# A four-stage transformer kernel on one core: a depth-routed layer written with overlapping batches, and the products of two rotary attention steps issued together

## The chip, the core and the metric

The kernel runs on one core of a Trainium2 chip. The metric is the device time of one execution in microseconds (us), lower is better. Six kinds of work appear in the profile: PE (TensorE's matmuls), PEld (TensorE's weight loads), DVE (VectorE), ACT (ScalarE), POOL (GpSimd) and SP, which issues the DMAs.

## What is computed

The input x is 4 sequences (B) of 1024 tokens (T) with 128 channels (D), float32. Four stages follow each other, each with a residual and a layer norm:

```python
x = layernorm(x + linear_attention(x))        # 16 heads
x = layernorm(x + switch_attention(x))        # 8 heads, 5 experts, top 3
x = layernorm(x + rotary_attention(x))        # 16 heads of 8 channels, full softmax
x = layernorm(x + depth_routed_ffn(x))

def depth_routed_ffn(x, w_r, b_r, W1, b1, W2, b2):
    weights = x @ w_r + b_r                    # one number a token
    threshold = top_k(weights, 512)[-1]        # per sequence
    selected = weights > threshold
    hidden = gelu(x @ W1 + b1)                 # 128 -> 512
    blk = hidden @ W2 + b2                     # 512 -> 128
    return where(selected, blk, x)
```

The change touches the third and the fourth stage only.

## The kernel before

Each stage is a function with its own block: all five engines run their own list of instructions, meet at its end, and POOL clears the stage's semaphores. The order on each engine is written out by hand; waits are semaphores.

**Rotary attention (`rotary_lead`).** A batch has 16 heads in groups of 4; a group has 2 pairs of heads and 8 key tiles, so a batch has 64 steps (pair and key tile `kt`) and the stage 256. A step has two score units (c = 0 and 1, one for each half of the queries). A score unit (L2072) is two matmuls for the two heads of the pair, each on 32 rows of the array, into one of three buffers `unit_b` of two PSUM banks each; score unit u goes where unit u-3 was, so it waits until ACT's exponential of unit u-3 is done. ACT's exponential (L2020) reads 128x1024 scores and writes `probs`, two buffers by step. The products of a step (L2087) are four matmuls on four column groups of the array (each recorded as two, so eight records), which read `probs` and add into the one bank `acc_b`. After 8 steps DVE copies `acc_b` (L2182), PE turns the copy (`turn`, L2099) and DVE divides. Between the steps lie "pieces" of the neighbouring batches: the projections q, k (with their swapped forms) and v of the next batch, each half a batch, and the transposition and output projection of the batch before. All of them use one bank, `piece_b`, which DVE must have read before the next piece is made. DVE normalizes the batch before (`norm`) right behind the last output projection. PE's order in a step is: score unit c=1 of this step, c=0 of the next, the products of the step before, then a turn or a piece, if one is due. The positions come from `PIECE_STEPS`, `TURN` and `NORM_AT`.

**Depth-routed layer (`depth_ffn`).** A loop over the 4 batches. SP loads the batch from the SBUF tensor `r1` into `xs` once more. PE transposes it (L2320), ACT copies it (`xT`, L2296), PE makes the router's row with the router vector repeated over 128 columns (L2326), ACT adds the bias (`w_row`, L2300), PE turns it into a column (L2339), and makes the hidden layer in four blocks (L2333), of which ACT takes the gelu (L2305). DVE counts, for each of 8 token tiles, how many weights are as large (L2366). PE makes the output channels by tokens (L2344), ACT adds the bias (L2307), PE transposes back (L2350), and DVE selects (L2382), normalizes (L66 to L85) and SP stores. The transposition of the next batch waits for ACT's L2307, and the counting of the next batch stands behind the norm of this one on DVE.

## Time and profile before

| | us |
|---|---|
| median of 3 runs (2033.87 to 2038.4) | 2034.81 |
| the profiled execution, its own time | 2035.62 |
| its span, first to last instruction | 2033.8 |
| rotary stage's exponentials, first start to last end | 514.8 |
| depth-routed layer, first load to the last store's issue | 112.3 |

The span is that of the profiled execution; 1.8 us lie around it. A time in a row counts from the span's start. In a timeline the first number is the start and the second the length of a merged stretch; what stands in brackets is how long the engine had been idle before it and what ended that.

### The profile page before, as it was taken

How to read it: one execution, taken by the hardware profiler on the slowest of the kernel's cores; microseconds unless marked ns; L12 is line 12 of the kernel's file. 1: busy time of each engine (PE TensorE's matmuls, PEld its weight loads, DVE VectorE, ACT ScalarE, POOL GpSimd, SP SyncE). 2: the span in 40 equal slices, each digit the busy share in tenths (PEclk: the TensorE clock that was granted, in tenths of full speed). 3: DMA queues.
4: the chain of work that ended last, by engine and by line, in shares of the span. 5: the costliest groups of instructions: out<-in, count | busy, mean ns of one | idle time of the engine just before them, and what ended most of it. 6: DMA issues, size and time to landing. Idle time of an engine off the chain costs nothing. (4 is left out here: it accounts for less than half of the span.)

```text
span 2033.8 us, 25515 instructions
## 1 busy us (share of the span) xinstructions
PE 1784.7 (88%) x8756; PEld 815.7 (40%) x8756; DVE 1163.4 (57%) x1924; ACT 1273.6 (63%) x2424; POOL 920.5 (45%) x512
## 2 busy tenths in 40 slices
PE   7888469999999999999999998529999999999386
PEld 3433245444545445554555552212333332333142
DVE  6998597986668776687765662331313223120287
ACT  1121215677676767767677677409999999999132
POOL 4566306788866788667887688400000000000000
PEclk8998689999999999999999999769999999999698
DMA  2000000000000000000000000022311212210011
GB/s 69 1 1 0 24 20 15 16 20 20 11 20 11 20 14 17 20 10 20 11 20 20 11 10 1 0 97 81 104 42 60 86 43 65 81 43 1 23 36 36
DMA packets 28808, 61.01 MB, mean 30 GB/s; under 512 B 4528, under 2 KB 15232, under 8 KB 28672
## 3 DMA queue, kind: packets, MB, share of 16 engines
q1 hardware_dynamic: 28672, 59.29, 9.0%
q8 instruction: 74, 1.21, 0.2%
q14 instruction: 62, 0.51, 0.1%
HBM read 38.31 MB, written 18.87 MB: 28 GB/s over the span
## 5 line engine op out<-in xcount | busy, mean ns | idle before, releaser
L707 POOL TENSOR_TENSOR b_psum<-b_psum,b_probs 128x1024 f32<-128x1024 f32 x192 | 460.7, 2400 | 172.4 <-ACT b_probs L847 165.8
L2020 ACT ACTIVATE c_probs<-banks 128x1024 f32<-128x1024 f32 x512 | 484.0, 1040 | 67.2 <-PE banks L2072 48.6
L1225 DVE TENSOR_TENSOR b_gated<-banks,b_g 128x480 f32<-128x480 f32 x512 | 314.2, 656 | 226.2 <-PE banks L949 221.3
L847 ACT ACTIVATE b_probs<-banks 128x1024 f32<-128x1024 f32 x256 | 254.2, 1019 | 216.1 <-PE banks L982 215.3
L949 PE MATMUL banks<-b_w,b_xh 128*128 128x480 f32 x1024 | 351.9, 398 | 33.4 <-DVE b_gated L1225 19.3
L1233 DVE TENSOR_REDUCE b_tok<-b_gated 128x192 f32<-128x960 f32 x256 | 281.5, 1139 | 0.5
L2087 PE MATMUL banks<-c_probs,c_vg 128*32 128x512 f32 x2048 | 273.9, 607 | 5.3 <-DVE c_acc L2182 3.5
L982 PE MATMUL banks<-b_qq,b_kk 64*128 64x512 f32 x1024 | 262.6, 622 | 14.2 <-DVE b_gated L1225 10.1
L818 ACT ACTIVATE b_share<-b_o,b_picked 128x64 f32<-128x64 f32 x1080 | 268.8, 339 | 0.0
L1014 PE MATMUL banks<-b_probs,b_tok 128*64 128x512 f32 x1024 | 252.4, 614 | 2.4 <-ACT b_probs L847 2.4
L949 PEld LDWEIGHTS banks<-b_w,b_xh 128*128 128x128 f32 x1024 | 194.3, 190 | 115.7 <-issue 39.6
L2004 POOL COPY c_vg<-c_v 128x64 f32<-128x64 f32 x64 | 12.3, 238 | 471.3 <-PE banks L2087 342.7
L2072 PE MATMUL banks<-c_queries,c_keys 32*128 32x512 f32 x1024 | 206.0, 468 | 18.9 <-DMA c_queries<-c_heads 17.2
L949 PE MATMUL banks<-b_w,b_xl 128*128 128x480 f32 x512 | 195.6, 382 | 0.0
L2072 PEld LDWEIGHTS banks<-c_queries,c_keys 32*128 32x128 f32 x1024 | 84.0, 184 | 219.0 <-ACT c_probs L2020 183.0
L718 POOL TENSOR_TENSOR b_z<-b_z,b_share 128x1280 f32<-128x1280 f32 x54 | 157.5, 2917 | 0.0
L1014 PEld LDWEIGHTS banks<-b_probs,b_tok 128*64 128x64 f32 x1024 | 62.8, 138 | 175.9 <-issue 143.6
L982 PEld LDWEIGHTS banks<-b_qq,b_kk 64*128 64x128 f32 x1024 | 87.2, 186 | 111.9 <-issue 59.4
L2182 DVE COPY c_acc<-banks 128x512 f32<-128x512 f32 x32 | 22.1, 691 | 191.1 <-PE banks L2087 190.9
L281 POOL TENSOR_TENSOR a_qscan<-a_scan,a_q 128x1024 f32<-128x1024 f32 x36 | 89.0, 2478 | 89.6 <-DVE a_scan L440 89.6
L707 POOL TENSOR_TENSOR b_psum<-b_probs 128x1024 f32<-128x1024 f32 x32 | 76.4, 2388 | 74.9 <-ACT b_probs L847 74.9
L399 PE MATMUL banks<-a_qscan,a_sel 128*128 128x512 f32 x128 | 73.3, 702 | 32.2 <-POOL a_qscan L281 32.1
(226 smaller groups left out, 1863.0 us busy)
## 6 DMA issues: line engine op xcount, KB each, us to landing
b_raw_w<-in_L_ffn_W SPq DMA_DIRECT2D x32, 480.0 KB, 3.2
c_heads<-c_split SPq DMA_DIRECT2D x24, 512.0 KB
c_keys<-c_heads SPq DMA_DIRECT2D x16, 512.0 KB, 3.8
c_queries<-c_heads SPq DMA_DIRECT2D x16, 512.0 KB, 5.1
c_heads<-c_split SPq DMA_DIRECT2D x8, 384.0 KB
a_xs<-in_L_attn_x SPq DMA_DIRECT2D x4, 512.0 KB, 8.3
d_xs<-r SPq DMA_DIRECT2D x4, 512.0 KB, 2.9
out<-d_yo SPq DMA_DIRECT2D x4, 512.0 KB, 3.2
```

The lines of the kernel that those rows point to most:

```text
L707: nc.gpsimd.tensor_tensor(psum[:, par, :], prev, probs[:, i % 4, :], ALU.add).then_inc(psum_rdy, 1)
L718: nc.gpsimd.tensor_tensor(zf, zf, sf, ALU.add).then_inc(z_rdy[half], 1)
L818: nc.scalar.activation(dst[:, e, :], o[:, t, :], ACT.Copy, scale=picked[:, b % 2, t, h * E + e:h * E + e + 1]).then_inc(share_rdy, 1)
L847: nc.scalar.activation(probs[:, i % 4, :], score_b[i % 2], ACT.Exp).then_inc(exp_rdy, 1)
L949: last = nc.tensor.matmul(proj_b[u % WAYS][:, 0:HALF_W], a[:, x_of % 2, t * P:(t + 1) * P], w[:, par, part, j, :], start=(i == 0), stop=(i ...
L982: last = nc.tensor.matmul(score_b[i % 2][:, lo:hi], kk[rows, par, (side + i) % 2, i // 2 * P:(i // 2 + 1) * P], qq[rows, par, :], start=Tr ...
L1014: last = nc.tensor.matmul(acc_b[DH * half:DH * half + DH, :], tok[:, n % 4, 2, i, :], probs[:, i % 4, lo:hi], start=(i == 0), stop=(i == N ...
L1225: nc.vector.tensor_tensor(shape(gated[:, t % 2, j, :]), shape(proj_b[u % WAYS][:, 0:HALF_W]), g.unsqueeze(2).broadcast_to([P, 3, HD2, E]), ...
L1233: nc.vector.tensor_reduce(tok[:, n % 4, :, t, :].rearrange("p j (f d) -> p f j d", f=2), gated[:, t % 2, :, :].rearrange("p f (j d e) -> p ...
L2020: nc.scalar.activation(probs[:, step % 2, c, :, :], unit_b[u % NU], ACT.Exp, scale=float(HD) ** -0.5).then_inc(exp_rdy, 1)
L2072: last = nc.tensor.matmul(unit_b[u % NU][:, s, :], keys[at:at + 32, par, kt * P:(kt + 1) * P], queries[at:at + 32, par, c * HALF:(c + 1) * ...
L2087: last = nc.tensor.matmul(acc_b[at:at + 32, :], vg[:, par, kt, 2 * pp + s, :], probs[:, kt % 2, half, s, :], start=(kt == 0), stop=(kt == ...
```

## The change

Rotary attention becomes `rotary_twos`: the products of two steps stand next to each other in PE's list, behind the score units of every even step; `probs` has four buffers where it had two; turns and pieces stand at odd steps; the norm of the batch before stands behind step 14.

```diff
@@ -1822,7 +1822,7 @@
-def rotary_lead(nc, x, out, ps, ident, I, flag, tag):
+def rotary_twos(nc, x, out, ps, ident, I, flag, tag):
@@ -1841,10 +1841,10 @@
-    TURN = 2
-    NORM_AT = 13
+    TURN = 3
+    NORM_AT = 14
-    PIECE_STEPS = [i + 1 if i % NT == TURN else i for i in range(3, 3 * (NZ + NX) + 3, 3)]
+    PIECE_STEPS = [i for i in range(5, STEPS * NG, 2) if i % NT != TURN][:NZ + NX]
@@ -1860,7 +1860,7 @@
-        probs = sb("probs", [P, 2, 2, 2, HALF])
+        probs = sb("probs", [P, 4, 2, 2, HALF])
@@ -2013,11 +2013,11 @@
-                act.wait_ge(pv_done, ONE + STEPS - 1 + step)
+                act.wait_ge(pv_done, ONE + STEPS - 3 + step)
-                    nc.scalar.activation(probs[:, step % 2, c, :, :], unit_b[u % NU], ACT.Exp, scale=float(HD) ** -0.5).then_inc(exp_rdy, 1)
+                    nc.scalar.activation(probs[:, step % 4, c, :, :], unit_b[u % NU], ACT.Exp, scale=float(HD) ** -0.5).then_inc(exp_rdy, 1)
@@ -2084,7 +2084,7 @@
-                        last = nc.tensor.matmul(acc_b[at:at + 32, :], vg[:, par, kt, 2 * pp + s, :], probs[:, kt % 2, half, s, :],
+                        last = nc.tensor.matmul(acc_b[at:at + 32, :], vg[:, par, kt, 2 * pp + s, :], probs[:, kt % 4, half, s, :],
@@ -2112,10 +2112,9 @@
-                    if i:
-                        products(b, i - 1)
-                    elif not first:
-                        products(b - 1, BS - 1)
+                    if i % 2 == 0 and step:
+                        for back in (2, 1):
+                            products(*((b, i - back) if i else (b - 1, BS - back)))
@@ -2123,7 +2122,8 @@
-            products(B - 1, BS - 1)
+            for back in (2, 1):
+                products(B - 1, BS - back)
```

The depth-routed layer becomes `depth_lead`, written out for the four batches. PE transposes straight from `r1`, without the load into `xs`. The transposition, the router's row and its column for batch b+1 stand between the hidden blocks of batch b; the router's column is eight transpositions of one row each. The output comes out as tokens by channels: the hidden layer is the stationary operand and W2 the moving one (32 matmuls of 128 columns where there were 8 of 512), so that the transposition back and ACT's bias pass are gone. POOL makes x times its weight plus b2 for the selected tokens (three passes over 128x1024, `keep`) and iterates the inverse roots for batches 0 to 2; ACT writes their normalized output. DVE counts for batch b+1 (`choose`) before it gathers batch b. Many buffers are doubled.

```diff
-def depth_ffn(nc, x, out_dram, ps, ident, I):
+def depth_lead(nc, x, out_dram, ps, ident, I):
...
+        piece_b = [ps[:, 0, :], ps[:, 1, :]]
+        hid_b = [ps[:, i:i + 2, :].rearrange("p a n -> p (a n)") for i in (2, 4)]
+        blk_b = [ps[:, 6, :], ps[:, 7, :]]
...
+            sp.dma_start(wr[:, :], I["L1_ffn_w_r"]).then_inc(r_in, 16)
+            sp.dma_start(br[:, :], I["L1_ffn_b_r"].rearrange("(o n) -> o n", o=1).broadcast_to([P, 1])).then_inc(r_in, 16)
+            sp.dma_start(w1[:, :], I["L1_ffn_W1"]).then_inc(w1_in, 16)
+            sp.dma_start(b1[:, :], I["L1_ffn_b1"]).then_inc(w1_in, 16)
+            sp.dma_start(b2[:, :], I["L1_ffn_b2"].rearrange("(o n) -> o n", o=1).broadcast_to([P, D])).then_inc(b2_in, 16)
+            sp.dma_start(w2[:, :, :], I["L1_ffn_W2"].rearrange("(n p) c -> p n c", p=P)).then_inc(w2_in, 16)
...
+            def keep(b):
+                if b == 0:
+                    pool.wait_ge(b2_in, 16)
+                pool.wait_ge(chosen, 2 * b + 2)
+                if b >= 2:
+                    pool.wait_ge(y_rdy, NT * (b - 1))
+                nc.gpsimd.tensor_tensor(kept[:, b % 2, :, :], x[:, b * NT:(b + 1) * NT, :], weight[:, b % 2, :].unsqueeze(2).broadcast_to([P, NT, D]), ALU.mult).then_inc(scaled, 1)
+                nc.gpsimd.tensor_tensor(shifts[:, :, :], b2[:, :].unsqueeze(1).broadcast_to([P, NT, D]), sel[:, b % 2, :].unsqueeze(2).broadcast_to([P, NT, D]), ALU.mult).then_inc(scaled, 1)
+                pool.wait_ge(scaled, 2 * b + 2)
+                nc.gpsimd.tensor_tensor(kept[:, b % 2, :, :], kept[:, b % 2, :, :], shifts[:, :, :], ALU.add).then_inc(kept_rdy, 1)
...
+            def inverse_roots(b):
+                pool.wait_ge(moments, MOMENT_STEPS * (b + 1))
+                st = Steps(pool, newton, NEWTON_STEPS * b)
+                var, half_step = tmp[:, 0, :], tmp[:, 1, :]
+                for _ in range(3):
...
+            keep(0)
+            for b in range(B):
+                if b + 1 < B:
+                    keep(b + 1)
+                    inverse_roots(b)
...
+            def hidden(b, n):
+                act.wait_ge(hid_ps, NB * b + n + 1)
+                if b and n == 0:
+                    act.wait_ge(blk_ps, 2 * b)
+                nc.scalar.activation(hid[:, n, :], hid_b[n % 2], ACT.Gelu, bias=b1[:, n:n + 1]).then_inc(hid_sb, 1)
...
+            def finish_norm(b):
+                act.wait_ge(newton, NEWTON_STEPS * (b + 1))
+                if b >= 2:
+                    act.wait_ge(out_done[b - 2], 16)
+                for t in range(NT):
+                    nc.scalar.activation(yo[:, b % 2, t, :], y[:, b % 2, t, :], ACT.Identity, bias=shift[:, t:t + 1], scale=rs[:, t:t + 1]).then_inc(normed, 1)
...
+            copy_x(0)
+            copy_rows(0)
+            act.wait_ge(w1_in, 16 * 2)
+            for b in range(B):
+                hidden(b, 0)
+                if b + 1 < B:
+                    copy_x(b + 1)
+                hidden(b, 1)
+                if b + 1 < B:
+                    copy_rows(b + 1)
+                hidden(b, 2)
+                hidden(b, 3)
+                if b:
+                    finish_norm(b - 1)
...
+            def turn_x(b):
+                for half in range(2):
+                    if b and half == 0:
+                        pe.wait_ge(col_sb, b)
+                    if b and half == 1:
+                        pe.wait_ge(row_sb, 2 * b)
+                    for j in range(4):
+                        last = nc.tensor.transpose(piece_b[half][:, j * P:(j + 1) * P], x[:, b * NT + 4 * half + j, :], ident[:, :])
+                    last.then_inc(turned, 1)
...
+            def router_column(b):
+                pe.wait_ge(row_sb, 2 * b + 2)
                 for t in range(NT):
-                    last = nc.tensor.transpose(tr_ps[:, t * P:(t + 1) * P], xs[:, t, :], ident[:, :])
-                last.then_inc(xT_ps, 1)
-                pe.wait_ge(xT_sb, b + 1)
-                pe.wait_ge(y_rdy, ONE + b)
+                    last = nc.tensor.transpose(piece_b[0][:, t:t + 1], w_row[0:1, b % 2, t * P:(t + 1) * P], ident[0:1, 0:1])
+                last.then_inc(col_ps, 1)
...
+            def contract(b):
+                if b == 0:
+                    pe.wait_ge(w2_in, 16)
+                pe.wait_ge(hid_sb, NB * b + NB)
+                for half in range(2):
+                    if b:
+                        pe.wait_ge(y_rdy, NT * (b - 1) + NT // 2 * (half + 1))
+                    for j in range(4):
+                        t = 4 * half + j
+                        for n in range(NB):
+                            last = nc.tensor.matmul(blk_b[half][:, j * P:(j + 1) * P], hid[:, n, t * P:(t + 1) * P], w2[:, n, :], start=(n == 0), stop=(n == NB - 1))
+                    last.then_inc(blk_ps, 1)
...
+            turn_x(0)
+            router_row(0)
+            router_column(0)
+            for b in range(B):
+                expand(b, 0)
+                if b + 1 < B:
+                    turn_x(b + 1)
+                expand(b, 1)
+                if b + 1 < B:
+                    router_row(b + 1)
+                expand(b, 2)
+                expand(b, 3)
+                if b + 1 < B:
+                    router_column(b + 1)
+                contract(b)
...
+            def choose(b):
                 dve.wait_ge(col_ps, b + 1)
-                nc.vector.tensor_copy(w_col[:, :], row_b.rearrange("p (t r) -> p t r", r=P)[:, :, 0]).then_inc(col_sb, 1)
+                nc.vector.tensor_copy(w_col[:, b % 2, :], piece_b[0][:, 0:NT]).then_inc(col_sb, 1)
                 dve.wait_ge(col_sb, b + 1)
+                dve.wait_ge(row_sb, 2 * b + 2)
+                if b:
+                    dve.wait_ge(chosen, 2 * b)
                 for t in range(NT):
-                    if t >= 2:
-                        dve.wait_ge(steps, b * V_STEPS + t - 1)
-                    st.done(nc.vector.tensor_scalar(ge[:, t % 2, :], w_row[:, :], w_col[:, t:t + 1], None, ALU.is_ge, ALU.add,
-                                                    accum_out=count[:, t:t + 1]))
+                    if NT * b + t >= 2:
+                        dve.wait_ge(counts, NT * b + t - 1)
+                    nc.vector.tensor_scalar(ge[:, t % 2, :], w_row[:, b % 2, :], w_col[:, b % 2, t:t + 1], None, ALU.is_ge, ALU.add,
+                                            accum_out=count[:, t:t + 1]).then_inc(counts, 1)
+                dve.wait_ge(counts, NT * (b + 1))
+                if b >= 2:
+                    dve.wait_ge(y_rdy, NT * (b - 1))
+                    dve.wait_ge(scaled, 2 * (b - 1))
+                nc.vector.tensor_scalar(sel[:, b % 2, :], count[:, :], float(K), None, ALU.is_lt).then_inc(chosen, 1)
+                dve.wait_ge(chosen, 2 * b + 1)
+                nc.vector.tensor_scalar(weight[:, b % 2, :], sel[:, b % 2, :], -1.0, 2.0, ALU.mult, ALU.add).then_inc(chosen, 1)
...
+            def gather(b, half):
+                dve.wait_ge(blk_ps, 2 * b + half + 1)
+                if half == 0:
+                    dve.wait_ge(kept_rdy, b + 1)
+                    dve.wait_ge(chosen, 2 * b + 1)
+                    if b >= 2:
+                        dve.wait_ge(normed, NT * (b - 1))
+                for j in range(4):
+                    t = 4 * half + j
+                    nc.vector.scalar_tensor_tensor(y[:, b % 2, t, :], blk_b[half][:, j * P:(j + 1) * P], sel[:, b % 2, t:t + 1], kept[:, b % 2, t, :], ALU.mult, ALU.add).then_inc(y_rdy, 1)
...
+            def moment_guess(b, st):
                 st.settle()
-                st.link(nc.vector.tensor_scalar(sel[:, :], count[:, :], float(K), None, ALU.is_lt))
-                st.link(nc.vector.tensor_scalar(keep[:, :], sel[:, :], -1.0, 2.0, ALU.mult, ALU.add))
-                dve.wait_ge(x_in, 16 * b + 16)
+                if b:
+                    dve.wait_ge(newton, NEWTON_STEPS * b)
+                    dve.wait_ge(normed, NT * b)
...
+            choose(0)
+            for b in range(B):
+                if b + 1 < B:
+                    choose(b + 1)
+                st = Steps(dve, moments, MOMENT_STEPS * b)
+                for half in range(2):
+                    gather(b, half)
+                    moment_stats(b, st, half)
+                moment_guess(b, st)
+            last_norm(B - 1)
...
-        depth_ffn(nc, r1, out_dram, ps, ident, I)
+        depth_lead(nc, r1, out_dram, ps, ident, I)
```

The places on which the prediction rests are all in PE's and DVE's lists. PE in the rotary stage, around a turn (c_queries and c_keys are the score units' operands, c_probs the products'), before:

```order
L2072 MATMUL banks<-c_queries,c_keys 128x512 x4
L2087 MATMUL banks<-c_probs,c_vg 32x512 x4
L2099 MATMUL banks<-ident,c_acc 128x128 x4
L2072 MATMUL banks<-c_queries,c_keys 128x512 x4
L2087 MATMUL banks<-c_probs,c_vg 32x512 x4
```

The same place in the changed kernel:

```order
L2087 MATMUL banks<-c_probs,c_vg 32x512 x8
L2072 MATMUL banks<-c_queries,c_keys 128x512 x4
L2099 MATMUL banks<-ident,c_acc 128x128 x4
L2072 MATMUL banks<-c_queries,c_keys 128x512 x4
L2087 MATMUL banks<-c_probs,c_vg 32x512 x8
L2072 MATMUL banks<-c_queries,c_keys 128x512 x8
```

A step's two score units and its products alternated; now eight product matmuls stand together, and between two such groups eight score matmuls, with a turn (or a piece) in their middle where one is due.

PE in the depth-routed layer, before, the loop's body from the last hidden block (d_xT, d_w) to the transposition back (REGISTER_ALU rows belong to waits against a counter):

```order
L2333 MATMUL banks<-d_xT,d_w 128x512 x2
L2344 MATMUL banks<-d_hid,d_w 128x512 x4
L2342 REGISTER_ALU
L2344 MATMUL banks<-d_hid,d_w 128x512 x2
L2342 REGISTER_ALU
L2344 MATMUL banks<-d_hid,d_w 128x512 x2
L2347 REGISTER_ALU
L2350 MATMUL banks<-ident,d_blk 128x128 x8
```

The changed kernel, batch 0 from its first hidden block to its output:

```order
L2412 MATMUL banks<-d_xT,d_w 128x512 x2
L2387 MATMUL banks<-ident,r 128x128 x8
L2412 MATMUL banks<-d_xT,d_w 128x512 x2
L2396 MATMUL banks<-d_xT,d_wr 128x512 x2
L2412 MATMUL banks<-d_xT,d_w 128x512 x4
L2402 MATMUL banks<-ident,d_w_row 128x1 x8
L2426 MATMUL banks<-d_w,d_hid 128x128 x32
```

L2387, L2396 and L2402 belong to the next batch; the output's matmuls (L2426) went from 8 to 32, and no transposition follows them.

DVE in the changed layer, its first rows:

```order
L2451 COPY d_w_col<-banks 128x8
L2459 TENSOR_SCALAR d_ge,d_count<-d_w_row,d_w_col 128x1024 x8
L2465 TENSOR_SCALAR d_sel<-d_count 128x8
L2467 TENSOR_SCALAR d_weight<-d_sel 128x8
L2479 SCALAR_TENSOR_TENSOR d_y<-banks,d_sel,d_kept 128x128 x4
L2487 BN_STATS d_stats<-d_y 128x6 x4
```

The first four rows come twice (batches 0 and 1) before the gathering of batch 0, which is cut here to its first half.

## Rows read from the trace of the kernel before

**Rows 1.** Busy times by engine in a stretch, then clock, DMA share, GB/s.

```profile
1924.00:2033.80 109.80, 82.17 (x240) 40.43 (x240) 81.84 (x284) 30.80 (x28) 0.00 (x0) 0.87 0.10 34
```

**Rows 2.** Timeline of ACT, rotary stage: start, length, exponentials in it.

```profile
1370.88 3.77 ACT L2020 ACTIVATE c_probs<-banks 128x1024 f32<-128x1024 f32 x4 [36.42 <-PE banks L2072]
...
1378.05 16.62 ACT L2020 ACTIVATE c_probs<-banks 128x1024 f32<-128x1024 f32 x18 [0.51 <-PE banks L2087]
...
1493.19 14.79 ACT L2020 ACTIVATE c_probs<-banks 128x1024 f32<-128x1024 f32 x16 [0.18 <-PE banks L2087]
...
1624.40 14.79 ACT L2020 ACTIVATE c_probs<-banks 128x1024 f32<-128x1024 f32 x16 [0.17 <-PE banks L2087]
```

**Rows 3.** Timeline of the last rotary batch, which holds no projections.

```profile
1863.25 14.79 ACT L2020 ACTIVATE c_probs<-banks 128x1024 f32<-128x1024 f32 x16 [0.18 <-PE banks L2087]
...
1865.24 0.18 PEld L2072 LDWEIGHTS banks<-c_queries,c_keys 32*128 32x128 f32 x2 [0.29 <-ACT c_probs L2020]
...
1865.67 1.07 PE L2087 MATMUL banks<-c_probs,c_vg 128*32 128x512 f32 x8
...
1878.21 7.44 ACT L2020 ACTIVATE c_probs<-banks 128x1024 f32<-128x1024 f32 x8 [0.16 <-PE banks L2087]
```

**Rows 4.** Timeline of batch 1, a turn and an output projection.

```profile
1522.22 0.66 PE L2099 MATMUL banks<-ident,c_acc 128*128 128x128 f32 x4
...
1522.80 0.73 PE L2072 MATMUL banks<-c_queries,c_keys 32*128 32x512 f32 x4
...
1524.46 0.73 PE L2072 MATMUL banks<-c_queries,c_keys 32*128 32x512 f32 x4
...
1525.12 1.06 PE L2087 MATMUL banks<-c_probs,c_vg 128*32 128x512 f32 x8
...
1526.12 1.16 PE L2057 MATMUL banks<-c_wo,c_aoT 128*128 128x128 f32 x8
1527.21 0.73 PE L2072 MATMUL banks<-c_queries,c_keys 32*128 32x512 f32 x4
...
1527.75 1.03 ACT L2020 ACTIVATE c_probs<-banks 128x1024 f32<-128x1024 f32 x1 [0.29 <-PE banks L2072]
```

**Rows 5.** Timeline of the switch stage, products on two column groups.

```profile
1104.78 1.94 PE L1014 MATMUL banks<-b_probs,b_tok 128*64 128x512 f32 x8
...
1106.64 3.04 PE L1053 MATMUL banks<-b_zT,b_wo 128*128 128x512 f32 x6
```

**Rows 6.** Timeline of DVE, the norm in batch 1: first and last part.

```profile
1528.04 1.65 DVE L66 BATCH_NORM_STATS2 c_stats<-c_y 128x6 f32<-128x128 f32 x8
...
1532.73 2.14 DVE L85 TENSOR_SCALAR r<-c_y,c_mv,c_rs 128x128 f32<-128x128 f32 x8
```

**Rows 7.** Groups of the depth-routed layer: busy, mean ns, idle before and releasers.

```profile
L2366 DVE TENSOR_SCALAR_CACHE_REDUCE d_ge<-d_w_row,d_w_col 128x1024 f32<-128x1024 f32 x32 | 38.7, 1275 | 0.1
L2333 PE MATMUL banks<-d_xT,d_w 128*128 128x512 f32 x64 | 28.8, 592 | 0.0
...
L2307 ACT ACTIVATE d_blk<-banks,d_b 128x1024 f32<-128x1024 f32 x4 | 4.5, 1114 | 23.0 <-PE banks L2344 23.0
```

**Rows 8.** Timeline of the depth-routed layer: its start, its end.

```profile
1916.47 0.57 SPq L2262 DMA_DIRECT2D d_xs<-r  x1
...
1924.19 1.96 PE L2320 MATMUL banks<-ident,d_xs 128*128 128x128 f32 x8 [17.43 <-POOL d_wr_rep L2287]
...
1927.25 3.44 PE L2326 MATMUL banks<-d_xT,d_wr_rep 128*128 128x512 f32 x4 [1.10 <-ACT d_xT L2296]
...
2028.73 0.39 SPq L2273 DMA_DIRECT2D out<-d_yo  x1
```

**Rows 9.** Timeline of the linear stage: POOL's inverse roots, ACT's normalized output.

```profile
149.43 0.20 POOL L267 TENSOR_TENSOR a_rs<-a_tmp,a_rs 128x8 f32<-128x8 f32 x1
149.72 2.16 POOL L264 TENSOR_TENSOR a_tmp<-a_rs 128x8 f32<-128x8 f32 x1
...
171.27 3.19 ACT L323 ACTIVATE r<-a_y,a_shift,a_rs 128x128 f32<-128x128 f32 x8
```

**Rows 10.** Group of POOL, rotary stage: one pass over 128x1024.

```profile
L1994 POOL TENSOR_TENSOR c_xb<-r,c_b_all 128x1024 f32<-128x1024 f32 x4 | 9.5, 2369 | 0.0
```

200 lines of the change are left out of this document (95 added, 105 removed).

## The prediction

> **What bounds the kernel now.** I read the page's slices first (which stages keep PE full), then the timelines of ACT and of PE in the two changed stages. The other two stages keep their instructions and get no term.
>
> In the rotary stage ACT is the slower engine as long as PE has only its steps: 16 exponentials stand back to back in 14.79 us [rows 3], and with the last one's 1.03 [rows 4] that is (14.79 - 1.03)/15 = 0.918 us each, 1.84 a step. PE needs less: two score units 0.66 (1524.46 to 1525.12), the products 1.00 (1525.12 to 1526.12), so 1.66 [rows 4]. The reader should see in [rows 3] that the second score unit of a step (1865.24) starts 0.05 after the second exponential ends (1863.25 + 0.918 + 1.03 = 1865.20): PE waits there for ACT. Where a projection stands between (1.09, from 1526.12 to 1527.21 [rows 4]) PE needs 2.75 and ACT waits. That is why 128 exponentials with projections take 131.2 us (1493.19 to 1624.40) [rows 2], and without them 16 take 14.96.
>
> The depth-routed layer is bound by no engine: PE is busy 82.2 of 109.8 us, DVE 81.8 [rows 1]. It is a chain, (2028.73 - 1924.19)/4 = 26 us a batch [rows 8]; ACT's bias pass alone waits 23.0 us in four rounds for PE's output [rows 7], and the count of the next batch (8 x 1.275, [rows 7]) stands behind the norm.
>
> **Rotary stage, the change.** Nothing is added but order and buffers. Two things follow.
>
> First, what PE saves. The products of one step are two passes over four column groups, 1.00. The nearest row for two steps together is a run of four passes over two column groups, 1104.78 to 1106.64 = 1.86 [rows 5], against 2 x 1.00. So a pass is (1.86 - 1.00)/2 = 0.43 and the change of array shape 0.14. The score side loses one change as well: four units in a row would take less than 2 x 0.66. I take 1.86 for the pair of products; bounds 1.72 (nothing but the streaming, 4 x 0.43) and 2.00 (two of today's).
>
> Second, what PE's list now makes ACT wait for. Follow the ring of three score buffers. Score unit u=2i+2 waits for exponential 2i-1. Behind it stand the products of two steps, and only then unit 2i+3. So from the start of exponential 2i-1 to the start of exponential 2i+3: 1.03 + 0.05 (end to score unit, above) + 0.43 (score unit to products, 1865.24 to 1865.67 [rows 3]) + 1.86 (products) + 0.54 (score unit to exponential, 1527.21 to 1527.75 [rows 4]) = 3.91 us for four exponentials, where ACT needs 4 x 0.918 = 3.67. Before, the same ring was 1.03 + 0.05 + 0.43 + 1.00 + 0.54 = 3.05 and hidden. The ring becomes the bound: I use 3.90, with bounds 3.76 and 4.04.
>
> A turn or a transposition (0.58, 1522.22 to 1522.80 [rows 4]) is hidden in it: 1.86 + 0.66 + 0.58 + 0.66 = 3.76 of PE. A projection (1.09) is not: 1.86 + 0.66 + 1.09 + 0.66 = 4.27, or about 4.24 for a q or k piece; 0.34 over the ring. There are 10 + 12 + 12 + 2 = 36 of these in the four batches: 12.2 us. The norm takes DVE 6.83 us (1528.04 to 1532.73 + 2.14) [rows 6], now behind the piece of step 13: the first transposition's copy then ends some 8.4 us after that piece, and PE comes to the second one (step 17), which needs the same bank, after about 7.1. That is 1.3 in each of three batches, 3.9. The slow start stays (six exponentials from 1370.88 to 1378.05 are 7.2 where 5.5 would do, 1.7 [rows 2]).
>
> Sum: 511 gaps = 127.75 x 3.90 = 498.2, + 1.0 (the last one) + 12.2 + 3.9 + 1.7 = 517.0 us, against 514.8 now (1370.88 [rows 2] to 1878.21 + 7.44 [rows 3]). The stage loses 2.2 us: what the projections cost less (131.2 a batch becomes about 130) is given back in the steps without them (119.7 a batch becomes 124.8). Bounds from the ring alone: -16 and +20.
>
> **Depth-routed layer, the change.** The new path, in the trace's time, if the block starts where it does (1916.47 [rows 8]):
> - The router's row needs the first two loads, not all seven. PE starts at 1924.19 today, when all have landed [rows 8]; the second load is issued about 1 us in. I take 1920.7 (between 1918 and 1924); the transposition (1.96 [rows 8]) lies ahead of it. Row 3.44 at the clock of [rows 8], ACT's half 0.6 (half of a 1.1 pass [rows 7]), column about 0.9 (an estimate, eight small transpositions): 1925.7.
> - To the first output: four hidden blocks at 1.73 (four passes of 0.43), transposition 1.09, row 1.73, then the last gelu 1.2 (a pass of that shape is 1.114 [rows 7]): 10.9. Contraction of batch 0 starts at 1936.6.
> - The contraction is 32 matmuls of 128 columns; the nearest row has four in 1.09 with a change of array shape in it [rows 4], so 8 x 0.9 = 7.3, at most 8 x 1.09 = 8.7 (now 6.9). A round of PE is 7.3 + 10.9 = 18.2. DVE needs 8 x 1.275 = 10.2 for a count [rows 7] and about 6 for the rest (the norm's 6.83 without its last 2.14 and the small steps, and 8 selections), POOL 3 x 2.37 [rows 10] + 14 x 0.29 [rows 9] = 11.2, ACT 4 x 1.1 + 4 x 0.6 + 3.2 = 10: PE bounds the round. Contraction of batch 2 starts at 1973.0, of batch 3 at 1988.4 (no next batch in it: 15.4).
> - The end hangs on the other engines. The count of batch 3 starts just before the contraction of batch 2 and ends at 1982.9; POOL's three passes to 1990.0, inverse roots of batch 2 to 1994 (I take 1996), ACT's eight writes 3.2 [rows 9]: 1999.2. Only then may DVE aggregate batch 3 (it gathered by 1998): aggregation and twelve small steps 3.1 (now 1528.04 + 1.65 to 1532.73 = 3.04 for nearly the same [rows 6]), ACT's four writes 1.7: 2004.0.
>
> The last store is issued at 2004.1 instead of 2028.73 [rows 8]: -24.6. Bounds: contraction at 8.7 and each POOL pass a third longer give -17, an earlier start -28.
>
> **Sum.** 2035.62 (the profiled execution's own time) - 24.6 + 2.2 = 2013.2. That execution lies 0.8 above the median of the runs, so about 2012.5; I say 2013.
>
> **Rivals.**
> - *The ring does not bind; PE's saving counts.* The stage would run at ACT's pace, and only the pairs with a projection at PE's: 470.1 (511 x 0.918 + 1) + 3.9 + 1.7 + 36 x 0.57 = 496.2, 18.6 less than now; 1992 in all. For it: the products' 1.00 has 0.14 beyond the two passes, and the score units' 0.66 some 0.2, once less in each pair. Against it: the wait at 1865.24 stands just there, and the ring hides only products of 3.67 - 2.05 = 1.62. The Trainium skill (TensorEngine Tiling, Key Properties) says that changing the tiling mode drains the engine; by that alone, fewer changes are a gain, and it says nothing of who waits for the scores in the meantime. 0.12.
> - *The products of two steps take twice what one takes* (2.00). Ring 4.04, + 17.9: 2031. Against it are [rows 5]. 0.10.
> - *Slower than before: POOL's small steps stall.* A 128x8 step takes 0.20 as a rule and once 2.16 [rows 9]. The round leaves POOL 18.2 - 11.2 = 7.0 us, 3.6 such stalls; beyond, each costs 1.96 on the way to ACT's writes and the next aggregation. The gain of 22.4 is spent by 11.4 more over three batches; with all 14 stalled in each of them the time is 2013 + 3 x (27.4 - 7.0) = 2074. Decides: more than some 7 of 14. Against it: DVE was scanning there, and here it compares one tensor with a column. The Trainium skill (SBUF — State Buffer) has the two engines block each other only where DVE reads two SBUF tensors or runs in a two-port mode, which speaks against it too. 0.06.
> - *The forecast*, with its terms within their bounds: 0.72, own range 2003 to 2024.
>
> **How the numbers follow.** About 0.2% (4 us) is what a measurement can tell here. The range 1996 to 2031 leaves out the first rival and the third. Faster holds the forecast, the first rival and nearly all of the second: 0.91; same 0.04 (second with the layer at -17); slower 0.05.
>
> **What would show it.** Right: products of L2087 with 16 records in some 1.9 us; exponentials in groups of four with about 0.2 idle before the fourth's successor, released by PE's scores; 16 of them in 15.6 us in the last batch (now 14.96), but a batch with projections near 130; contractions 18 us apart, last store issued about 88 us after the stage's start. Wrong: ACT back to back in the last batch (first rival); POOL steps of 2 us on the chain (third); an output contraction over 9 us; a lower granted clock in the rotary stage, where PE will pause near 0.9 us in each pair of steps.

## The result, and the profile after

The changed kernel takes 2012.72 us (median of 4 runs, 2010.14 to 2014.0); the kernel before took 2035.43 in runs beside it. The ratio is 0.9885 with a 95% interval from 0.987 to 0.9899: 1.15% faster. The forecast was 2013. The profiled execution took 2014.0 us, with a span of 2012.1, 21.7 less than before.

ACT in the rotary stage, the changed kernel (start, length, exponentials in the stretch, in brackets the idle time ahead of it):

```profile
1372.41 6.52 ACT L2020 ACTIVATE c_probs<-banks 128x1024 f32<-128x1024 f32 x7 [36.80 <-PE banks L2072]
1380.58 19.37 ACT L2020 ACTIVATE c_probs<-banks 128x1024 f32<-128x1024 f32 x20 [1.65 <-PE banks L2072]
...
1519.96 11.57 ACT L2020 ACTIVATE c_probs<-banks 128x1024 f32<-128x1024 f32 x12 [0.28 <-PE banks L2072]
...
1649.47 11.56 ACT L2020 ACTIVATE c_probs<-banks 128x1024 f32<-128x1024 f32 x12 [0.28 <-PE banks L2072]
...
1799.09 86.83 ACT L2020 ACTIVATE c_probs<-banks 128x1024 f32<-128x1024 f32 x89 [0.40 <-PE banks L2072]
```

The stage's 512 exponentials last from 1372.41 to 1885.92 (1799.09 + 86.83), 513.5 us; before they lasted 514.8 ([rows 2, 3]). A batch is 129.5 (1519.96 to 1649.47) where it was 131.2. Executions differ by more than the 1.3 us of the stage: the same rotary stage took 513.5 to 516.2 us in six profiles (here, e1, e8, e9, e10, e12), the old one 514.8 and 515.0 (before, e2). In the part of the last batch that holds no projections, 89 exponentials take 86.83, so 16 take 15.6 where they took 14.96 [rows 3]. PE in that batch, a pair of steps with a turn in it:

```profile
1843.08 0.50 PE L2072 MATMUL banks<-c_queries,c_keys 32*128 32x512 f32 x2 [0.65 <-ACT c_probs L2020]
1843.51 1.92 PE L2087 MATMUL banks<-c_probs,c_vg 128*32 128x512 f32 x16
1845.36 0.73 PE L2072 MATMUL banks<-c_queries,c_keys 32*128 32x512 f32 x4
1846.02 0.66 PE L2099 MATMUL banks<-ident,c_acc 128*128 128x128 f32 x4
```

The reader should see that the score unit at 1843.08 waits for ACT, and that behind it PE gives 1.85 us (1843.51 to 1845.36) to the products before it makes the next one. PE has become the less loaded engine. The two rows give its busy time first, ACT's as the fourth and the granted clock as the sixth number, in the last batch before and after:

```profile
1779.00:1885.00 106.00, 104.72 (x710) 32.30 (x708) 16.93 (x65) 103.35 (x112) 3.94 (x9) 1.00 0.06 21
1779.00:1886.00 107.00, 94.73 (x699) 32.92 (x698) 16.42 (x65) 102.83 (x109) 4.17 (x9) 1.00 0.06 21
```

The clock stayed at 1.00 although PE now pauses in each pair, so that sign of being wrong did not come.

The depth-routed layer, PE and the last of the other engines, from a timeline (the pieces of SP are DMA issues):

```profile
1917.45 0.35 SPq L2264 DMA_DIRECT2D d_wr<-in_L_ffn_w_r  x1
...
1920.73 3.78 PE L2396 MATMUL banks<-d_xT,d_wr 128*128 128x512 f32 x4 [1.16 <-DMA d_br<-in_L_ffn_b_r]
...
1926.23 3.78 PE L2412 MATMUL banks<-d_xT,d_w 128*128 128x512 f32 x4
1929.81 1.91 PE L2387 MATMUL banks<-ident,r 128*128 128x128 f32 x8
1931.51 2.35 PE L2412 MATMUL banks<-d_xT,d_w 128*128 128x512 f32 x4
...
1999.37 1.12 DVE L2479 SCALAR_TENSOR_TENSOR d_y<-banks,d_sel,d_kept 128x128 f32<-128x128 f32 x4 [1.54 <-PE banks L2426]
...
2004.53 1.65 ACT L2374 ACTIVATE d_yo<-d_y,d_shift,d_rs 128x128 f32<-128x128 f32 x4 [4.61 <-DVE d_shift L2511]
...
2006.61 0.51 SPq L2277 DMA_DIRECT2D out<-d_yo  x1
```

From the first load's issue to the last store's it is 89.2 us; it was 112.3 [rows 8]. In the chain that ended last, the four contractions (L2426) stand where PE starts each of them:

```profile
1940.31 7.38 PE banks L2426 x64
...
1957.19 1.12 ACT d_hid L2347
1958.36 7.41 PE banks L2426 x64
...
1976.43 7.41 PE banks L2426 x64
...
1991.92 7.43 PE banks L2426 x64
```

A round is 18.05 us. The chain runs through PE, with one gelu in each round, and not through DVE or POOL until the last gather; but DVE is idle for only some 1.6 us of a round, so DVE's own list is close behind as a limit. The 21.7 us of the span are: 23.1 from the layer, 1.3 from the exponentials, and against them 1.5 ahead of the first exponential (1372.41 for 1370.88), 0.7 between the last one and the layer, and 0.4 behind the last store (the parts are rounded). Some of this belongs to the execution and not to the change: in eight other profiles of the new layer in this order (e2 to e7, e11 and e12) it took 85.6 to 87.7 us where this one shows 89.2.

### The profile page after: what moved, and what is told of

It is laid out like the page before. It is cut to its first block and busy times, and to the rows that moved or that the text cites. A ratio compares the mean times of both kernels' runs of the same rounds, so it can differ in the third digit from the quotient of the medians.

```text
span 2012.1 us, 25633 instructions
## 1 busy us (share of the span) xinstructions
PE 1750.1 (87%) x8916; PEld 836.6 (42%) x8916; DVE 1149.1 (57%) x1834; ACT 1280.4 (64%) x2456; POOL 953.7 (47%) x565
## 5 line engine op out<-in xcount | busy, mean ns | idle before, releaser
L949 PE MATMUL banks<-b_w,b_xh 128*128 128x480 f32 x1024 | 353.3, 399 | 33.5 <-DVE b_gated L1225 19.4
L982 PE MATMUL banks<-b_qq,b_kk 64*128 64x512 f32 x1024 | 263.7, 625 | 14.7 <-DVE b_gated L1225 10.0
L2087 PE MATMUL banks<-c_probs,c_vg 128*32 128x512 f32 x2048 | 247.7, 601 | 0.3 <-DVE c_acc L2182 0.2
L2072 PE MATMUL banks<-c_queries,c_keys 32*128 32x512 f32 x1024 | 191.4, 464 | 49.8 <-ACT c_probs L2020 31.9
L2072 PEld LDWEIGHTS banks<-c_queries,c_keys 32*128 32x128 f32 x1024 | 79.7, 183 | 217.9 <-ACT c_probs L2020 183.7
```

Of the source, the lines that this page charges most:

```text
L949: last = nc.tensor.matmul(proj_b[u % WAYS][:, 0:HALF_W], a[:, x_of % 2, t * P:(t + 1) * P], w[:, par, part, j, :], start=(i == 0), stop=(i ...
L982: last = nc.tensor.matmul(score_b[i % 2][:, lo:hi], kk[rows, par, (side + i) % 2, i // 2 * P:(i // 2 + 1) * P], qq[rows, par, :], start=Tr ...
L2072: last = nc.tensor.matmul(unit_b[u % NU][:, s, :], keys[at:at + 32, par, kt * P:(kt + 1) * P], queries[at:at + 32, par, c * HALF:(c + 1) * ...
L2087: last = nc.tensor.matmul(acc_b[at:at + 32, :], vg[:, par, kt, 2 * pp + s, :], probs[:, kt % 4, half, s, :], start=(kt == 0), stop=(kt == ...
```

## The experiments

All ratios are to the kernel before, run on the same chip in the same job; its medians were 2037.19, 2038.74 and 2037.60 us in the three jobs.

| kernel | us | ratio, 95% interval |
|---|---|---|
| e1_rotary_alone | 2039.98 | 1.0014, 1.0002 to 1.0025 |
| e2_depth_alone | 2012.26 | 0.9883, 0.986 to 0.9906 |
| e3_twice_before | 2046.28 | 1.0031, 1.0011 to 1.005 |
| e4_twice_middle | 2025.49 | 0.9932, 0.991 to 0.9954 |
| e5_single_four | 2006.16 | 0.9838, 0.9815 to 0.9861 |
| e6_norm_late | 2012.0 | 0.9867, 0.9851 to 0.9884 |
| e7_mixed | 2013.67 | 0.9881, 0.9864 to 0.9898 |
| e8_no_lead | 2036.77 | 0.9985, 0.9974 to 0.9996 |
| e9_count_behind | 2025.13 | 0.9939, 0.9924 to 0.9954 |
| e10_router_ahead | 2026.94 | 0.9943, 0.9928 to 0.9959 |
| e11_four_late | 2001.48 | 0.9827, 0.9813 to 0.984 |
| e12_after_again | 2014.2 | 0.9876, 0.986 to 0.9892 |

### Each part alone

The kernel before with the new rotary function:

```diff
-        rotary_lead(nc, r2, r1, ps, ident, I, flag, "c_")
+        rotary_twos(nc, r2, r1, ps, ident, I, flag, "c_")
         depth_ffn(nc, r1, out_dram, ps, ident, I)
```

> The kernel before with the changed rotary stage alone; the depth-routed layer stays as it was. Theory (the ring of three score buffers bounds the stage at 3.90 us a pair of steps, which gives back what the projections cost less): no change that can be measured, 2034 us, the exponentials again over some 513.5 us. Rival (PE's saved changes of array shape are a gain of the whole change): 2016 us.

And with the new depth-routed layer:

```diff
         rotary_lead(nc, r2, r1, ps, ident, I, flag, "c_")
-        depth_ffn(nc, r1, out_dram, ps, ident, I)
+        depth_lead(nc, r1, out_dram, ps, ident, I)
```

> The kernel before with the changed depth-routed layer alone; the rotary stage stays as it was. Theory: all of the gain, 2012.5 us, the last store issued 89 us after the layer's first load. Rival (a part of the gain belongs to the rotary stage): 2018 us or more.

2039.98 and 2012.26 us. By the ratio the rotary part costs 0.14%, 2.8 us beside the kernel before on the same chip, with an interval from 0.4 to 5. In e1's profile the stage itself takes 516.0 us, 1.2 more than before, and 2.9 lie ahead of the stage, in code that the change doesn't touch; so that 2.8 is near the forecast of 2.2 is partly chance. The layer is the whole gain (85.7 us in e2's profile). The rival in which PE's saving counts is gone. e1 came out 6 us above its expectation: 2.5 are its longer slow start (below), and the kernel before was some 2 slower on this chip than in the first runs; the rest is not settled.

### Where the rotary stage's ring runs

A score unit computed a second time right behind itself costs PE some 0.23 us. In e3 it is the one that stands ahead of the products, within the ring of three score buffers that the prediction drew; in e4 the one in the middle, outside of it.

```diff
-                for s in range(2):
+                for s in (0, 1, 0, 1) if c == 0 and step % 2 == 1 else (0, 1):
```

> The changed kernel with one score unit of each pair of steps computed twice into the same banks: the one right ahead of the two products (the same result, 0.22 us more of PE). It lies inside the ring from an exponential's end over the products to the next score unit. Theory (ring): the ring grows from 3.90 to 4.12 in all 128 pairs, + 28 us, 2041 us. Rival (ACT bounds the stage, or PE does with slack): under + 10 us. If PE's total work bounds the stage, this run and the next cost the same.

```diff
-                for s in range(2):
+                for s in (0, 1, 0, 1) if c == 0 and step % 2 == 0 else (0, 1):
```

> The changed kernel with another score unit of each pair computed twice: the second one behind the products, before the turn or piece. The same 0.22 us of PE, outside the ring. Theory (ring): nothing in pairs without a projection, 0.22 in the 36 with one and about 0.08 in those with a turn, + 10 us, 2023 us; the last batch stays at 15.6 us for 16 exponentials. Rival (PE's total work bounds the stage): + 28 us like the run before.

Timelines of ACT in the last batch, first e3, then e4:

```profile
1875.44 3.77 ACT L2020 ACTIVATE c_probs<-banks 128x1024 f32<-128x1024 f32 x4 [0.36 <-PE banks L2072]
1879.58 3.77 ACT L2020 ACTIVATE c_probs<-banks 128x1024 f32<-128x1024 f32 x4 [0.37 <-PE banks L2072]
```

```profile
1865.82 15.47 ACT L2020 ACTIVATE c_probs<-banks 128x1024 f32<-128x1024 f32 x16 [0.22 <-PE banks L2072]
1881.51 15.48 ACT L2020 ACTIVATE c_probs<-banks 128x1024 f32<-128x1024 f32 x16 [0.22 <-PE banks L2072]
```

The same matmuls, inside the ring, make a pair of steps 4.14 us (1875.44 to 1879.58), 0.24 over the 3.90; outside of it 3.92 (1865.82 to 1881.51, a quarter). By the ratios e3 costs some 30 us over the changed kernel (0.0146 x 2037) and e4 some 10, against 28 and 10 expected. What e4 costs it costs where projections stand, since there PE's own work sets the pace. (Each profile also has one wait of 2 to 2.5 us behind the norm, with PE at its lower clock, that the changed kernel's has not.) So away from the projections it is the ring that paces the stage: shown.

### Single products with four buffers, and the norm's place

e5 has the new layer, but issues the products after every step, as before, and has the turns, the pieces and the norm where they were before. Of the rotary change it keeps the four buffers (the edit is shown against the kernel before):

```diff
-        probs = sb("probs", [P, 2, 2, 2, HALF])
+        probs = sb("probs", [P, 4, 2, 2, HALF])
-                act.wait_ge(pv_done, ONE + STEPS - 1 + step)
+                act.wait_ge(pv_done, ONE + STEPS - 3 + step)
```

> The changed kernel's depth-routed layer, but in the rotary stage the products are issued after every step again, as before the change, with four buffers for the exponentials' results in place of two. The theory (the pair's products stand between two score units and so make the ring of three score buffers 3.90 us per two steps; single products leave it at 3.05, hidden by ACT's 3.67, and what is left of a loss before the change is the wait of each turn's exponential for a buffer, 0.28) expects 16 exponentials of the last batch in about 14.7 us (15.6 in the changed kernel, 14.96 before), the batches with projections between 127 and 131 us, and 1997 to 2006 us in all. The rival (the order of the products is not what paces the stage, 0.975 us per exponential is ACT's own pace there or the score units') expects 15.6 and the changed kernel's time, 2012.

It took 2006.16 us. ACT in its last batch:

```profile
1801.78 81.69 ACT L2020 ACTIVATE c_probs<-banks 128x1024 f32<-128x1024 f32 x89 [1.83 <-PE banks L2072]
```

89 exponentials in 81.69 us (86.83 in the changed kernel): 0.918 each, ACT's own pace, with no wait at a turn. Against e2, which differs from it in the two buffers alone, the ratio falls from 0.9883 to 0.9838, some 9 us, though the intervals just touch; in the two profiles the exponentials of the stage take 509.2 instead of 515.0, so 6 us are seen in the stage. The buffers were the useful half of the rotary change, and the order of the products, with the places that it needs, took back what they gave. The time lies just above the range's upper end; the row shows 1.83 us lost behind the norm, for which e6 and e11 were made. PE waits only 1.11 us there, for DVE's copy, and then works at its lower clock (a step's products take 1.94 us for 1.06). e6 is the changed kernel with

```diff
-    NORM_AT = 14
+    NORM_AT = 46
```

> The changed kernel with the norm of the finished batch on DVE at step 46 of a batch in place of step 14, where no turn or transposition waits for DVE's copies any more. The theory (the norm makes a transposition's copy late and PE waits 1.57 us for it in each of three batches) expects the three waits gone and 4 to 5 us less than the changed kernel: 2008. The rival (PE's wait is covered by the ring of score buffers all the same) expects 2012.

2012.0 us, its ratio 0.9867 against 0.9885 and 0.9876 for the changed kernel: no gain that can be told. The wait at the norm (PE's 1.57 us, in two of the three batches and not in all three as I had expected) is gone, and e6's batch shrinks to 128.1 us, but its start was slower by nearly as much. Timeline of ACT in e6, its start and one point of batches 1 and 3:

```profile
1373.22 6.52 ACT L2020 ACTIVATE c_probs<-banks 128x1024 f32<-128x1024 f32 x7 [36.77 <-PE banks L2072]
1382.18 3.77 ACT L2020 ACTIVATE c_probs<-banks 128x1024 f32<-128x1024 f32 x4 [2.44 <-PE banks L2072]
1387.81 12.74 ACT L2020 ACTIVATE c_probs<-banks 128x1024 f32<-128x1024 f32 x13 [1.85 <-PE banks L2072]
...
1523.29 11.57 ACT L2020 ACTIVATE c_probs<-banks 128x1024 f32<-128x1024 f32 x12 [0.27 <-PE banks L2072]
...
1779.52 11.57 ACT L2020 ACTIVATE c_probs<-banks 128x1024 f32<-128x1024 f32 x12 [0.27 <-PE banks L2072]
```

The batch is (1779.52 - 1523.29)/2. The start loses 2.44 + 1.85 where the profile of the changed kernel shows 1.65. This difference is not e6's own: the unaltered kernel, profiled again in e12, has it too (2.43 and 1.78), and e1 has it. Against e12's profile, with the same start, e6's exponentials take 513.0 for 516.2 us: the norm's place is worth some 3 us, which the ratios can't tell. PE stands still for 17.24 us (for a DMA of c_queries, 17.2 in e6) ahead of its first score units and makes them and the first products at the lower of its two clocks (granted 0.50). In the changed kernel's profile the higher one is there in the first pair's products (16 records in 3.15 us), in e6 only in the second pair's (3.64, then 3.36), and with it the start varies by 2.6 us.

e7 keeps the pairs while pieces are due and issues single products from step 46 (in the last batch from step 14) on:

```diff
+    SINGLE_FROM, SINGLE_LAST = 46, 14
...
-                    if i % 2 == 0 and step:
-                        for back in (2, 1):
-                            products(*((b, i - back) if i else (b - 1, BS - back)))
+                    for done in due(step):
+                        products(done // BS, done % BS)
```

> The changed kernel with the products issued in pairs only while turns, transpositions and projections are still due in a batch (steps up to 45; in the last batch up to 13), and one step at a time after that, with the four buffers as they are. The theory (a pair pays where PE is the slower engine, which is where a projection stands between, and costs where ACT is) expects the last batch at 14.7 us per 16 exponentials from its step 14 on, 50 steps x 0.11 = 5.5 us less there, and 3 x 18 steps x 0.11 = 6 us less in the other batches: about 2000 to 2002 us. The rival (single products give nothing back) expects 2012.

It took 2013.67: a miss by 12 us. The end of its last batch is as expected, 87 exponentials in 79.85 us:

```profile
1798.95 1.94 ACT L2036 ACTIVATE c_probs<-banks 128x1024 f32<-128x1024 f32 x2 [4.80 <-PE banks L2088]
1801.97 1.94 ACT L2036 ACTIVATE c_probs<-banks 128x1024 f32<-128x1024 f32 x2 [1.08 <-PE banks L2088]
1805.92 79.85 ACT L2036 ACTIVATE c_probs<-banks 128x1024 f32<-128x1024 f32 x87 [2.01 <-PE banks L2088]
```

But 7.9 us are lost ahead of it (4.80 + 1.08 + 2.01), and what stands on DVE and then on PE there says why:

```profile
1791.11 4.17 DVE L85 TENSOR_SCALAR r<-c_y,c_mv,c_rs 128x128 f32<-128x128 f32 x8
1795.42 0.69 DVE L2197 COPY c_acc<-banks 128x512 f32<-128x512 f32 x1
```

```profile
1796.26 1.94 PE L2103 MATMUL banks<-c_probs,c_vg 128*32 128x512 f32 x8 [4.30 <-DVE c_acc L2197]
```

The single products come to the next group earlier and need the bank `acc_b`, which DVE copies only behind the norm, and the norm's last part is twice as long as usual (4.17 where it is 2.14 [rows 6]). PE idles 4.30 us and then runs three steps at the lower clock (granted 0.50 from 1796.20 to 1802.00; 8 records of products in 1.94 where they take 1.06 [rows 4]). That is more than the 5.1 us which the single products give behind it. In the other batches, too, ACT lost 1.7 to 2.2 us three times because PE's products ran at the lower clock, which the changed kernel's profile shows nowhere behind its start: twice behind the norm (2.23 at 1539.85, where the changed kernel has 0.58) and once in batch 2, after PE had paused only 0.41 and 0.42 us:

```profile
1631.74 3.50 PE L2103 MATMUL banks<-c_probs,c_vg 128*32 128x512 f32 x16
```

```profile
1631.70:1635.00 3.30, 3.30 (x18) 0.51 0.00 0
```

The last row is PE alone, with the granted clock, 0.51, behind its busy time. e11 takes e5, with the norm's place changed:

```diff
-    NORM_AT = 13
+    NORM_AT = 43
```

> The kernel of e5_single_four (single products, four buffers, 2006.2 us) with the norm on DVE at step 43 of a batch, where the pieces are done. The theory (in each of three batches the norm makes PE wait for DVE's copy, ACT loses 1.8 to 2.8 us there, and PE runs at half clock for a step after it) expects 5 to 7 us less than e5_single_four: 1999 to 2001 us. The rival (the slow start or another wait takes it back, as in e6_norm_late) expects 2005 to 2006.

2001.48 us, ratio 0.9827: the fastest of the study, some 10 us under the changed kernel in the same job by the ratios (0.0049 x 2037.6), 12.7 by the medians. The exponentials of the stage last 505.8 us. Over e5 it is 4.7 us by the medians and only 2.2 by the ratios, whose intervals overlap, so how much of it is the norm's place stays open (the stage's exponentials: 505.8 for 509.2). The wait of 1.83 is gone from the last batch, but in two others the norm now delays a projection of v (PE):

```profile
1600.51 1.13 PE L2055 MATMUL banks<-c_wv,c_xT 128*128 128x128 f32 x8 [1.47 <-DVE c_v L2151]
```

### What of the layer's change brings the gain

e8 takes the lead away on PE and ACT alone (ACT's edit, not shown, puts its copies for the next batch behind its four gelu passes):

```diff
-                expand(b, 0)
-                if b + 1 < B:
-                    turn_x(b + 1)
-                expand(b, 1)
-                if b + 1 < B:
-                    router_row(b + 1)
-                expand(b, 2)
-                expand(b, 3)
-                if b + 1 < B:
-                    router_column(b + 1)
-                contract(b)
+                for n in range(NB):
+                    expand(b, n)
+                contract(b)
+                if b + 1 < B:
+                    turn_x(b + 1)
+                    router_row(b + 1)
+                    router_column(b + 1)
```

> The changed kernel, but in the depth-routed layer the next batch's transposition, router row and column come after the contraction of the batch in PE's list, and ACT's copies for them after the four hidden blocks. Everything else of the change stays. The theory (a round is 18.05 us of PE's work with the router between the hidden blocks, where it fills PE's waits for ACT) expects PE to wait for ACT's last hidden block and then for the router's copies, a round of some 20.5 us, and 2012 + 3 x 2.5 = 2019.5 us; so of the layer's 23 us some 7 come from the lead and some 16 from the rest (the first loads, no transposition back with ACT's bias pass, the norm off DVE's way). The rival (the lead is what brought all of the 23 us) expects 2030 or more; a second rival (the round hangs on DVE and POOL, and PE has room) expects 2012.

2036.77 us: the whole gain is gone, as the first rival had it, and my theory of this experiment fell. PE's contractions, from its timeline:

```profile
1960.79 9.93 PE L2423 MATMUL banks<-d_w,d_hid 128*128 128x128 f32 x64 [4.50 <-DVE d_y L2472]
...
1986.79 8.92 PE L2423 MATMUL banks<-d_w,d_hid 128*128 128x128 f32 x64 [4.42 <-DVE d_y L2472]
```

A round is 26.0 us (the two others 23.5 and 25.1), and the contraction waits for DVE's gather of the batch before. It is also longer itself, 9.93 us for 7.4, at a granted clock of 0.73. I had left out DVE's list: it counts batch b+1 before it gathers batch b. With the router's column behind the contraction, that count can only start after it, and the gather, and with it the next contraction, stands behind the count. The chain of work of that kernel shows the circle:

```profile
1948.58 0.67 PE banks L2399 x8
...
1949.47 9.70 DVE d_ge L2452 x16
...
1959.52 1.14 DVE d_y L2472 x4
1960.79 9.93 PE banks L2423 x64
```

So e8 measures a bad mixture and not "no lead". e9 takes the lead away on DVE too, and puts POOL's roots for batch b ahead of its three passes for batch b+1:

```diff
                 if b + 1 < B:
+                    inverse_roots(b)
                     keep(b + 1)
-                    inverse_roots(b)
...
             for b in range(B):
-                if b + 1 < B:
-                    choose(b + 1)
                 st = Steps(dve, moments, MOMENT_STEPS * b)
...
                 moment_guess(b, st)
+                if b + 1 < B:
+                    choose(b + 1)
```

> The kernel of e8_no_lead, which took 2036.8 us, with one thing more: DVE's count of batch b+1 and ACT's and POOL's work follow the old order, that is DVE gathers batch b, takes its moments and starts its norm, and only then counts batch b+1; POOL takes the inverse roots of b before its three passes of b+1. The new theory (in e8_no_lead a round was 26.0 us because the count of b+1, 9.7 us, could only start after the contraction of b and stood ahead of the gather of b, for which the next contraction waits) expects the round to be DVE's and POOL's ring instead: count 10.2, POOL's passes 6.2, gather and moments 6.6, together 23.0 us; last store some 14 us later than in the changed kernel, 2026 to 2028 us in all. The rival (the round hangs on PE's router standing behind the contraction, whatever DVE's order) expects 2036, as e8_no_lead.

And e10 keeps the lead on PE and ACT and takes it from DVE and POOL; it has this edit without e8's:

> The changed kernel with PE's and ACT's order as it is (the router of b+1 between the hidden blocks of b), but on DVE the count of b+1 behind the gather and the moments of b, as before the change, and POOL's inverse roots of b ahead of its passes of b+1. The theory (what the lead buys is that DVE can count the next batch under PE's contraction; PE's order alone is worth next to nothing) expects the ring of DVE and POOL, 23.0 us a round, and 2026 to 2029 us in all, as e9_count_behind. The rival (PE's order is what counts, DVE's count finds room anyway) expects 2012 to 2016.

2025.13 and 2026.94 us: the two are the same, though e10 has PE's new order. DVE's gathers in e10:

```profile
1968.31 1.13 DVE L2479 SCALAR_TENSOR_TENSOR d_y<-banks,d_sel,d_kept 128x128 f32<-128x128 f32 x4 [6.35 <-POOL d_kept L2295]
...
1989.92 1.13 DVE L2479 SCALAR_TENSOR_TENSOR d_y<-banks,d_sel,d_kept 128x128 f32<-128x128 f32 x4 [6.36 <-POOL d_kept L2295]
```

The round is 21.6 us (1968.31 to 1989.92), a circle of DVE and POOL: the count, POOL's three passes, gather and moments; DVE waits 6.4 us in it for POOL. e9's gathers are 21.6 to 22.2 us apart, in the same circle. I had expected 23.0; the gather and the moments take 4.9 us where I had 6.6, and the count 9.7 for 10.2. From the first load's issue to the last store's these kernels need:

| PE's router ahead | DVE's count and POOL's passes ahead | layer, us |
|---|---|---|
| yes | yes (after, e12; e2 to e7 and e11) | 89.2, 87.7; 85.6 to 87.7 |
| yes | no (e10) | 100.9 |
| no | yes (e8) | 112.6 |
| no | no (e9) | 99.7 |
| (before) | | 112.3 |

Neither order is worth anything alone, and one of them alone costs 13 us in the profiles (9 by the ratios). Together they bring 10.5 to 14 by this table (11 to 13 by the ratios of e9 against the changed kernel, e2 and e12), and the rest of the change (no load of x, the router ahead of the other loads, no transposition back with ACT's bias pass, the norm's roots on POOL and its writes on ACT) brings 12.6, from one profile each. How that splits further was not tried.

### The changed kernel again

> The changed kernel itself, unaltered, beside the others on the same chip, so that e9_count_behind to e11_four_late are read against it: 2012 to 2015 us by every theory.

2014.2 us, 0.9876. Its layer took 87.7 us where the first profile shows 89.2. In the first profile the window from the first load to the first contraction has a granted clock (the third number from the end) of 0.67; in e12's it is 0.72 (1922.70 to 1944.10), and in e2's, where the first contraction starts 19.4 us after the first load, 0.82:

```profile
1917.40:1940.30 22.90, 20.16 (x56) 10.39 (x57) 10.82 (x21) 10.62 (x13) 3.51 (x2) 0.67 0.12 30
1917.98:1937.40 19.42, 16.77 (x56) 8.41 (x57) 10.68 (x21) 10.52 (x13) 0.46 (x1) 0.82 0.13 35
```

## Why the prediction was right

That the median came within 0.3 us of 2013 is partly luck: in the profiled execution the layer gave 1.5 less than forecast, the rotary stage cost 3.5 less, and 2.6 were lost outside of both, which no term had; and each of these moves by 2 to 4 us from one execution to the next.

**The layer** was forecast at -24.6 and came at -23.1 (-24.6 to -26.7 in the eight other profiles). Its mechanism is shown by e2 and e8 to e10: the lead on PE and DVE together lets PE set the round, 18.05 us (forecast 18.2). Two sizes in it were off, and one wait. The first contraction starts 22.9 us after the first load instead of 20.1: the prediction costed the four hidden blocks, transposition and row of the first batch at the higher clock, and PE ran the first block and the transposition at the lower one (3.58 us, 1926.23 to 1929.81, for 1.73; 1.70 for the 1.09 of the prediction) and part of the second block, some 3.1 in all, while the router's column came 0.4 earlier than forecast. This size belongs to the execution: the same window is 19.3 to 21.4 us in the eight other profiles. POOL's passes take 1.90, 1.90 and 2.35 instead of 3 x 2.37. The wait is the last one: the end did not hang on POOL's roots and ACT's writes, as the step "the end hangs on the other engines" put it. PE finished the last contraction at 1999.35, and DVE's second gather, at 1999.37, waited for it alone. From the last contraction's start to the last store it is 14.7 us instead of 15.7. (The contraction's "8 x 0.9 = 7.3" is 7.2; it takes 7.4.)

**The rotary stage** was forecast at +2.2 and came at -1.3 (+1.4 in e12's profile of the same kernel). The pair of products is 1.85 (forecast 1.86), the ring 3.90, and both are shown, the ring by e3, e4 and e5. The term that was most mis-sized is the projections' 12.2 us. The forecast gave each pair with a projection 0.34 over the ring. Two in three have that; every third takes 0.10. It stands where the two score units ahead of it belong to different pairs of heads, on different rows of the array, and these two take 0.43 us where two of one pair take 0.66 (PE, changed kernel; the starts count):

```profile
1435.75 0.51 PE L2072 MATMUL banks<-c_queries,c_keys 32*128 32x512 f32 x4
1436.18 1.12 PE L2047 MATMUL banks<-c_xT,c_wk 128*128 128x512 f32 x2
1437.24 0.73 PE L2072 MATMUL banks<-c_queries,c_keys 32*128 32x512 f32 x4
```

So the 36 cost 24 x 0.34 + 12 x 0.10 = 9.4, 2.8 less. The norm's stall was forecast at 1.3 in each of three batches, 3.9. PE waits 1.57 us in two of them and not in the third; against e6, where this wait is gone, the batches are 1.4, 1.4 and 0.3 longer, so it cost 3.1, 0.8 less. The two make the forecast 3.6 too high; it was 3.5 too high in this execution. The slow start is 1.65, forecast 1.7, in this execution; in e12 it is 2.43 and 1.78, and there the longer start fills what the two terms had too much.

**The rivals.** That the ring does not bind (1992) is refuted by e3 and by the last batch. What it promised is real, but it needs single products: e5 and e11 get part of it. Products at 2.00 us: measured 1.85. POOL's small steps: each took 0.20 to 0.24 us, the 14 of a batch 3.9, and none stalled.

The step that I would now do otherwise is not in the prediction but in e8's expectation: I followed PE's list round the loop and not DVE's.

## What to carry to other kernels

When a batch's work is moved ahead of another's, it has to be moved on every engine in the circle: here PE's half alone brought nothing, and without it DVE's half made rounds of up to 26 us. Grouping products to save changes of array shape lengthens the time between two score units; count the ring of score buffers, as (exponential + handovers + products) per so many exponentials, against ACT's own pace, before grouping. A deeper result buffer and a place for the norm where nobody waits for DVE were worth more than the grouping (e11; how much each of the two gave is not settled).

## What the runs showed of the hardware

A DVE step of the kind TENSOR_SCALAR, from SBUF to SBUF, waited for a POOL pass that reads two full SBUF tensors. In the changed kernel, one of three batches, POOL and DVE:

```profile
1953.92 2.35 POOL L2295 TENSOR_TENSOR d_kept<-d_kept,d_shifts 128x1024 f32<-128x1024 f32 x1
...
1954.57 1.73 DVE L2498 TENSOR_SCALAR d_tmp<-d_mv 128x8 f32<-128x8 f32 x1
```

The DVE step ends at 1956.30, 0.03 behind the pass (1956.27), and so it does in the two other batches (1.68 and 1.60 us); in the last batch, with POOL idle, it takes 0.17. e7's long norm fits this too: one of its eight writes (L85), 1792.40 to 1794.76, took 2.37 us where the middle one took 0.34, and POOL's pass over two SBUF tensors ran from 1792.28 to 1794.68 there.

```profile
L85 DVE TENSOR_SCALAR r<-c_y,c_mv,c_rs x8: 334/339/2366, 1791.1 to 1794.9; 128x128 f32<-128x128 f32 x8
```

DVE's gathers out of PSUM and its moments ran beside POOL's first two passes, and its aggregation beside the third, at their usual length. The Trainium skill (SBUF — State Buffer, SBUF: two separate sides) has a port pair that the two engines lock for a whole instruction, which DVE needs in a two-port mode or for two SBUF inputs. The traces agree: POOL's pass had started first, and DVE waited for its end. In which mode DVE was, no run here shows. In the changed kernel it cost nothing on the chain; in e7 it cost 2 us just where PE waited.

PE's clock is the second thing. After 17 us of waiting ahead of the rotary stage PE worked at its lower clock (granted 0.50), and when the higher came differed between two executions of one kernel. Behind a short wait the clock sometimes falls and sometimes does not: PE waits 1.57 us for the same copy in the changed kernel and in e7, and then works at a granted clock of 1.00 in the one (1535.00 to 1543.00) and of 0.52 in the other (1535.80 to 1539.30). In the rotary stage behind its start the changed kernel's two profiles have no such fall, e5's has two and e7's four.
